# A graph network's gather stages: DVE reads one operand from PSUM beside the gathers, and POOL copies its own index columns

## The reference

```python
x = _layernorm(x + L0(x, ...)); x = _layernorm(x + L1(x, ...))
x = _layernorm(x + L2(x, ...)); x = _layernorm(x + L3(x, ...))
# L0, twice, with loops added: x = 0.5 * segment_sum(norm[:, None] * x[src], dst, n) + 0.5 * h; then relu, @ w1.T + b1, @ w2.T + b2
# L1: d_e = segment_sum(ones, he_idx, M);  d_v = segment_sum(hyperedge_weight[he_idx], node_idx, n)
#     he_feat = segment_sum(x_prime[node_idx], he_idx, M) * (hyperedge_weight / d_e)[:, None]
#     out = segment_sum(he_feat[he_idx], node_idx, n) * d_v_inv_sqrt[:, None];  return out @ W.T + b     (node_idx = src, he_idx = dst)
# L2: side = segment_sum(edge_weight[:, None] * emb[dst], src, n);  return (emb + 3 * side) / 4
# L3: edge scores from x[src], x[dst] and edge_attr, softmax over all edges, local[src] -= alpha * x[dst]
```

## Time and profile before

| | us |
|---|---|
| median of 3 runs (lowest, highest) | 8925.08 (8912.57, 8938.14) |
| the profiled execution | 8925.21 |
| its span | 8923.4 |
| PE busy | 4351.0 |
| PEld busy (beside PE) | 3221.3 |
| DVE busy | 3499.0 |
| ACT busy | 1201.9 |
| POOL busy | 5327.6 |
| POOL in the gathers of L368 | 3720.2 |

### The profile page before, as it was taken

How to read it: one execution, slowest core, us unless ns; L and a number is a source line. 1 busy time by engine, 2 the same in 40 slices (tenths; PEclk the granted TensorE clock), 3 DMA queues, 4 the chain that set the end, 5 groups by cost and what they waited for, 6 DMA issues and landing times. The chain is left out here.

```text
span 8923.4 us, 102562 instructions
## 1 busy us (share of the span) xinstructions
PE 4351.0 (49%) x17220; PEld 3221.3 (36%) x17221; DVE 3499.0 (39%) x11515; ACT 1201.9 (13%) x4632; POOL 5327.6 (60%) x5326
## 2 busy tenths in 40 slices
PE   6455554555543333145555555543333335666665
PEld 3333332333333323133333333322222224666654
DVE  8444444332232222141122222343333355666666
ACT  0000000000000000120000000010000024444443
POOL 0566675777776666626666666646666625555551
PEclk5555555555555555565555555555555558888886
DMA  9111111111111111161111211121111123333332
GB/s 159 52 45 46 44 46 45 45 46 46 45 45 45 46 44 45 42 38 45 45 44 45 45 44 45 45 42 44 44 44 44 43 48 93 96 98 99 98 94 40
DMA packets 665641, 492.66 MB, mean 55 GB/s; under 512 B 515113, under 2 KB 565684, under 8 KB 665476
## 3 DMA queue, kind: packets, MB, share of 16 engines
q0 software_dynamic: 183232, 378.81, 16.5%
q1 hardware_dynamic: 482228, 112.18, 7.6%
q10 hardware_dynamic: 144, 1.28, 0.1%
HBM read 411.96 MB, written 79.95 MB: 55 GB/s over the span
## 5 line engine op out<-in xcount | busy, mean ns | idle before, releaser
L368 POOL DMA_INDIRECT gathered<-node_table,idx x3696 | 3720.2, 1007 | 2151.6 <-issue 1124.8
L387 PE MATMUL ps<-onehots,gathered 128*128 128x128 f32 x4128 | 1618.6, 498 | 1484.4 <-DMA gathered<-node_table,idx 1336.3
L387 PEld LDWEIGHTS ps<-onehots,gathered 128*128 128x128 f32 x4128 | 1029.4, 312 | 2073.3 <-DMA gathered<-node_table,idx 1940.5
L389 PE MATMUL ps<-onehots,gathered 128*128 128x128 f32 x3264 | 1066.4, 470 | 1423.4 <-DVE agg L454 669.0
L389 PEld LDWEIGHTS ps<-onehots,gathered 128*128 128x128 f32 x3264 | 771.4, 319 | 1719.1 <-issue 907.3
L410 DVE TENSOR_TENSOR onehots<-iota,off_t 128x512 f32<-128x512 f32 x736 | 508.9, 693 | 2220.6 <-PE ps L387 1083.9
L923 POOL DMA_INDIRECT gathered<-node_table_xq,idx x832 | 796.1, 957 | 738.5 <-issue 225.9
L613 POOL DMA_INDIRECT bucketed_edges<-edge_rows,idx x782 | 775.6, 992 | 403.0 <-issue 253.1
L454 DVE TENSOR_TENSOR agg<-agg,ps 128x128 f32 x1632 | 466.9, 286 | 707.0 <-issue 608.7
L662 PE MATMUL ps<-gathered 128*128 128x49 f32 x1568 | 346.1, 414 | 681.9 <-DVE gathered L647 529.6
L662 PEld LDWEIGHTS ps<-gathered 128*128 128x128 f32 x1568 | 338.1, 332 | 689.8 <-DVE gathered L647 534.5
(11 more groups left out here) (258 smaller groups left out, 4482.7 us busy)
## 6 DMA issues: line engine op xcount, KB each, us to landing
gathered<-node_table,idx POOLq DMA_INDIRECT x3696
bucketed_edges<-edge_rows SPq DMA_DIRECT2D x52, 544.0 KB
edge_rows<-bucketed_edges SPq DMA_DIRECT2D x208, 128.0 KB
edge_rows<-in_edge_attr_dram SPq DMA_DIRECT2D x192, 128.0 KB
gathered<-node_table_xq,idx POOLq DMA_INDIRECT x832
bucketed_edges<-edge_rows,idx POOLq DMA_INDIRECT x782
node_table<-t_nodes SPq DMA_DIRECT2D x3, 3136.0 KB
node_table<-x_nodes SPq DMA_DIRECT2D x1, 3136.0 KB
```

The costliest lines, as they stand in the source:

```text
L368: nc.gpsimd.indirect_dma_start(g[:, k, :], None, table, bass.IndirectOffsetOnAxis(m.idx[:, k:k + 1], 0)).then_inc(S["landed"][k], 16)
L387: last = nc.tensor.matmul(m.ps[:, q, 0:P], g[:, k, :], m.oh[:, k, :], start=e == 0, stop=e == G - 1)
L389: last = nc.tensor.matmul(m.ps[:, q, e * P:(e + 1) * P], g[:, k, :], m.oh[:, k, :], start=True, stop=True)
```

## The change

DVE's operations beside the gathers read one of their two tensors from PSUM. `aggregate` copies `iota` once into the last 128 columns of bank 7, and L410 reads it there. In hop1 the hyperedges' weights are copied into banks 2 to 7 before the loop and read there by the side work, with a second load of the windows' starts into registers for it, clamped to M (written once per round, next to L424); PE then has two banks for its sums in place of four (`NS`). In hop2 the scan reads its ones from bank 7 and writes its running sum to banks 4 and 5, from where the predicated copy reads it.

ACT has no part in the loop any more. POOL casts eight index columns at a time itself (`stage`), twice per iteration, for the half that comes next: ahead of the fifth gather of each half it waits for `used` to say that PE has done the quarter four gathers back, and at the start of each half for its own copy. The clamp of the members' indices is computed once ahead of the stage, into `m.start`. The remaining hunks (sizes of a few tensors, and a loop register, `made`, that is now worked out where it is used) follow from this and are left out.

```diff
...
-def window_starts(nc, engine, m, at, count):
-    return nc.values_load_multi_w_load_instructions(m.startI[0:1, bass.ds(at, count)], engines=[engine], min_val=0, max_val=PARK,
-                                                    skip_runtime_bounds_check_because="clamped to PARK")[1]
+def window_starts(nc, engine, m, at, count, most=PARK):
+    return nc.values_load_multi_w_load_instructions(m.startI[0:1, bass.ds(at, count)], engines=[engine], min_val=0, max_val=most,
+                                                    skip_runtime_bounds_check_because="clamped to it")[1]
...
-def aggregate(nc, m, a, name, table, idx, dst_order, iters, weight=None, side=None, last_he=False, meta=None):
+def aggregate(nc, m, a, name, table, idx, dst_order, iters, weight=None, side=None, meta=None):
     off, NQ = m.off, U // G
+    NS = side.sums if side else NQ
     g = m.gather[:, 0:U * D].rearrange("p (t d) -> p t d", d=D)
-    with phase(nc, name, f"landed*{U} idx_ready used onehot added round dve side picked reg meta") as (S, block):
+    with phase(nc, name, f"landed*{U} idx_ready used onehot added round dve side picked meta") as (S, block):
         def iterations(eng):
             if isinstance(iters, int):
...
                                  a.bucketed[t0 * P:(t0 + n) * P, DE:DE + 3].rearrange("(t p) d -> p t d", p=P)).then_inc(S["meta"], 16)
                 sp.wait_ge(S["meta"], 16 * META)
-        @block.scalar
-        def _(act):
-            def body(t0, n, nt, i, made):
-                for q in range(NQ):
-                    cols, here = bass.ds(t0 + G * q, G), slice(G * q, G * q + G)
-                    act.wait_ge(S["used"], n * NQ + q + 1)
-                    if last_he:
-                        nc.scalar.activation(m.clampf[:, here], idx[:, cols], ACT.Relu, scale=-1.0, bias=m.lasthe[:, 0:1]).then_inc(S["reg"], 1)
-                        act.wait_ge(S["reg"], n * NQ + q + 1)
-                        nc.scalar.activation(m.idx[:, here], m.clampf[:, here], ACT.Identity, scale=-1.0,
-                                             bias=m.lasthe[:, 0:1]).then_inc(S["idx_ready"], 1)
-                    else:
-                        nc.scalar.copy(m.idx[:, here], idx[:, cols]).then_inc(S["idx_ready"], 1)
-            loops(act, body)
         @block.gpsimd
         def _(pool):
-            def body(t0, n, nt, i, made):
-                for q in range(NQ):
-                    hold(pool, S["idx_ready"], n * NQ + q + 1)
-                    for k in range(G * q, G * q + G):
+            pool.sem_inc(S["idx_ready"], 1)
+            def stage(t0, h):
+                cols, here = bass.ds(t0 + HALF * h, HALF), slice(HALF * (h % 2), HALF * (h % 2) + HALF)
+                nc.gpsimd.tensor_copy(m.idx[:, here], idx[:, cols]).then_inc(S["idx_ready"], 1)
+            def head(r, n):
+                if n is not None:
+                    hold(pool, S["idx_ready"], n * 2 + r + 1)
+                    hold(pool, S["used"], n * NQ + 2)
+                stage(0, 0)
+            def body(t0, n, nt, i, r):
+                for h in range(2):
+                    hold(pool, S["idx_ready"], n * 2 + r + h + 2)
+                    for k in range(HALF * h, HALF * h + HALF):
+                        if k == HALF * h + G:
+                            hold(pool, S["used"], n * NQ + 2 * h + 4)
+                            stage(t0, h + 1)
                         nc.gpsimd.indirect_dma_start(g[:, k, :], None, table,
                                                      bass.IndirectOffsetOnAxis(m.idx[:, k:k + 1], 0)).then_inc(S["landed"][k], 16)
-            loops(pool, body)
+            loops(pool, body, head)
         @block.tensor
         def _(pe):
             pe.sem_inc(S["used"], NQ)
-            def body(t0, n, nt, i, made):
+            def body(t0, n, nt, i, r):
                 for k in range(U):
                     q, e = k // G, k % G
                     if e == 0:
-                        pe.wait_ge(S["onehot"], made + q + 1)
+                        pe.wait_ge(S["onehot"], (n + r) * NQ + q + 1)
                         if dst_order:
                             pe.wait_ge(S["added"], n * NQ + q + 1)
                         else:
                             pe.wait_ge(S["added"], nt + G * q + G)
                     pe.wait_ge(S["landed"][k], nt + 16)
                     if dst_order:
-                        last = nc.tensor.matmul(m.ps[:, q, 0:P], g[:, k, :], m.oh[:, k, :], start=e == 0, stop=e == G - 1)
+                        last = nc.tensor.matmul(m.ps[:, q % NS, 0:P], g[:, k, :], m.oh[:, k, :], start=e == 0, stop=e == G - 1)
                     else:
                         last = nc.tensor.matmul(m.ps[:, q, e * P:(e + 1) * P], g[:, k, :], m.oh[:, k, :], start=True, stop=True)
                     if e == G - 1:
...
         @block.vector
         def _(v):
             V = nc.vector
-            a0 = NQ if dst_order else U
+            a0 = NS if dst_order else U
             v.sem_inc(S["added"], a0)
             step = chain(v, S["dve"])
+            step(V.tensor_copy(m.ps[:, 7, 512 - P:512], m.iota[:, :]))
             if side:
                 side.before(v, step, S)
             if dst_order:
...
                 here = m.oh[:, G * q:G * q + G, :]
                 if weight is None:
-                    V.tensor_tensor(here, m.iota[:, :].unsqueeze(1).to_broadcast([P, G, P]),
+                    V.tensor_tensor(here, m.ps[:, 7, 512 - P:512].unsqueeze(1).to_broadcast([P, G, P]),
                                     off[:, bass.ds(t0 + G * q, G)].unsqueeze(2).to_broadcast([P, G, P]), ALU.is_equal).then_inc(S["onehot"], 1)
                     return
                 for e in range(G):
...
                 if dst_order:
                     gs = m.glast[:, :]
                     V.tensor_scalar(gs, m.gstart[:, :], m.shift[:, 0:1], float(PARK), ALU.add, ALU.min).then_inc(S["round"], 1)
-                    v.wait_ge(S["round"], r * 4 + 1)
+                    v.wait_ge(S["round"], r * 5 + 1)
                     V.tensor_copy(m.startI[0:1, 0:NG], gs[0:1, :]).then_inc(S["round"], 1)
+                    V.tensor_scalar(m.startI[0:1, NG:2 * NG], gs[0:1, :], float(M), None, ALU.min).then_inc(S["round"], 1)
                     V.tensor_tensor(off[:, 0:NT].rearrange("p (t g) -> p t g", g=G), m.dst[:, 0:NT].rearrange("p (t g) -> p t g", g=G),
                                     gs.unsqueeze(2).to_broadcast([P, NG, G]), ALU.subtract).then_inc(S["round"], 1)
                     V.tensor_scalar(m.shift[:, :], m.shift[:, :], float(WIN), None, ALU.add).then_inc(S["round"], 1)
-                    hold(v, S["round"], r * 4 + 4)
+                    hold(v, S["round"], r * 5 + 5)
                 for q in range(NQ):
                     if dst_order:
                         v.wait_ge(S["used"], n * NQ + q + 1)
                     onehots(0, q)
-            def body(t0, n, nt, i, made):
+            def body(t0, n, nt, i, r):
                 if dst_order:
                     start = window_starts(nc, mybir.EngineType.DVE, m, i * NQ, NQ)
                 else:
                     start = window_starts(nc, mybir.EngineType.DVE, m, t0, U)
                 if side:
-                    for q in range(NQ):
-                        side.quarter(v, n, q, start[q], made, S)
+                    side.quarters(v, n, i, (n + r) * NQ, S)
                 for q in range(NQ):
                     v.wait_ge(S["used"], n * NQ + q + 1 + NQ)
...
                     if dst_order:
                         v.wait_ge(S["added"], n * NQ + q + a0)
                         w = m.agg[:, bass.ds(start[q], WIN)]
-                        V.tensor_tensor(w, w, m.ps[:, q, 0:P], ALU.add).then_inc(S["added"], 1)
+                        V.tensor_tensor(w, w, m.ps[:, q % NS, 0:P], ALU.add).then_inc(S["added"], 1)
                         continue
                     for e in range(G):
                         v.wait_ge(S["added"], nt + G * q + e + a0)
...
     def __init__(self, nc, m):
         self.nc, self.m = nc, m
+        self.sums = 2
+        self.cols = M + WIN
+        self.hw = m.ps[:, 2:8, :].rearrange("p b n -> p (b n)")[:, 0:self.cols]
     def before(self, v, step, S):
-        pass
-    def quarter(self, v, n, q, start, made, S):
+        m, V = self.m, self.nc.vector
+        for k in range(0, self.cols, 512):
+            w = min(512, self.cols - k)
+            step(V.tensor_copy(self.hw[:, k:k + w], m.side[:, k:k + w]))
+    def quarters(self, v, n, i, made, S):
         m, V, NQ = self.m, self.nc.vector, U // G
-        v.wait_ge(S["onehot"], made + q + 1)
-        V.tensor_tensor(m.junk[:, :, :], m.oh[:, G * q:G * q + G, :],
-                        m.side[:, bass.ds(start, WIN)].unsqueeze(1).to_broadcast([P, G, WIN]), ALU.mult).then_inc(S["picked"], 1)
-        v.wait_ge(S["picked"], n * 2 * NQ + 2 * q + 1)
-        V.tensor_reduce(m.picked[:, G * q:G * q + G], m.junk[:, :, :], AX.X, ALU.add).then_inc(S["picked"], 1)
```

(24 more changed lines are left out.)

19 lines of the change are left out of this document (9 added, 10 removed).

## The result

| | before | changed |
|---|---|---|
| median us (lowest to highest) | 8919.26 (8888.58 to 8938.14) | 8944.39 (8932.29 to 8963.0) |
| ratio, 95% interval | | 1.0026 (1.0019 to 1.0033) |
| ratio in a second comparison (run `after_again`) | | 1.0006 (0.9996 to 1.0016) |
| profiled span | 8923.4 | 8946.5 |

The account below looks back on a forecast made before the run. POOL's gathers were taken to bound the kernel: a 4609 us floor, 220 us of stretch, 539 us of pauses. The terms, -210 + 92 + 0 + 0 + 40 + 8 = -70 us, gave 8855 us, range 8480 to 9180.

Parts of the forecast that it names:

- What bounds the kernel: In the five gather stages, POOL's 3696 gathers set a floor of 4609 us, with stretched gathers and pauses above it.
- stretch: Gathers in the five stages taking longer than 0.947 us, mostly beside DVE operations with two SBUF tensors: 220 us together.
- pauses: POOL's waits for ACT's index copy in the five stages, less each stage's long first wait: 539 us in 165 waits.
- part 1: One-hots, weight products and scan read one tensor from SBUF, so gathers are no longer stretched: -210 us.
- rival C: In the gather stages something sets the pace; pauses grow by what the stretch loses: 8925 to 8990 us, chance 0.17.
- The copies: POOL's 462 index copies between gathers, 0.2 us each by a memset row, bounds 0.1 and 0.5: +92 us.
- ACT out of the loop: ACT's 0.19 us index copy leaves the path, but POOL's own wait, copy and issue take about as long: 0 us.
- The closer waits: POOL waits mid-half for PE's gather 4 places back, leaving 2.6 us of slack of some 13: 0 us.
- Rival B: Late signals to POOL end by themselves, so POOL stands up to 10 us longer each time: 9150 us, chance 0.20.
- hop2 loses a relief: In hop2 the scan's 1.4 us stops of POOL let things catch up; without them 0 to +74, taken +40 us.
- Once per stage: Copies of weights before hop1's first one-hot, copies of iota and two operations on the windows: +8 us.
- Rival D: Moving DVE's operands to PSUM does not free the gathers: 8855 + 210 = 9065 us, chance 0.05.

Follow-up runs that it names:

- after_again: The changed kernel unaltered, run again on the same chip as another run for comparing stages: 8943.09 us, 1.0006 of the kernel before.
- e1_psum_reads_only: The changed kernel with ACT's index copies and waits put back, so only the PSUM operands differ from the kernel before: 8939.13 us, ratio 1.0008.
- e2_pool_copies_only: The changed kernel with operands back in SBUF and four sums in hop1, so only POOL's index copies and their waits differ from before: 8934.81 us, ratio 1.0008.
- e5_wait_ten_back: The changed kernel, but POOL copies four columns per quarter, waiting for the quarter that ended 10 gathers back, not 4: 8921.89 us, ratio 0.9996.

## Why the prediction was wrong, point by point

- **What bounds the kernel** was half right. POOL's gathers are where the time is, but 4609 us of gathers, 220 of stretch and 539 of pauses are not three terms that can be taken away one by one. The last two are one term, what a pace of about 1.44 us a gather leaves over POOL's own work. The failing step is the sum of part 1: the stretch was sized right (211.7 us measured, 210 forecast) and priced as if it were on the path alone. `e1_psum_reads_only` shows it by itself: 223 us less in the gathers, 231 us more in the waits. The prediction had named the sign, a sum of pauses that moves by more than 100 us: POOL's waits went from 539 to 665 us, and with the gaps that the profile calls issue it was 209 us more.
- The page's numbers had said so. I wrote under rival C that the time per gather was about 1.44 us in hop1 and hop2 in spite of very different shares, and gave it 0.17. It was 1.448, 1.436, 1.434, 1.462 and 1.495 us in the five stages, while the stretch went from 0.6 to 124 us. Rival C, 8925 to 8990 us, is what came (8944), with a smaller price for the copies.
- **The copies** were 3 times too dear: 0.06 us each where nothing is late, 28 us in all, not 92, and below the lower bound of 0.1 too; in `e2_pool_copies_only`, with its copies and its stretch, the median is 7 us above the one before, which isn't clear of noise. The memset row gave the duration (0.13; the cast takes 0.19), but most of it fits into the issue gap, which I had put into the lower bound and not into the value.
- **ACT out of the loop**, 0: nothing speaks against it, and no run isolates it; `e1_psum_reads_only`, with ACT back in the loop and no copies on POOL, is at 1.0008 where the changed kernel is at 1.0026 and 1.0006. **The closer waits**, 0: right within 0.1 to 0.3%, which `e5_wait_ten_back` is faster than the changed kernel. The reason given, that running dry ends the delay, fits the traces and isn't proved by them. Rival B falls: by it each pause was to be up to 10 us longer, and the pauses got shorter, 3.7 us at most in hop1 where they were 5.6, and more frequent.
- **hop2 loses a relief**: right in kind, too small. Its waits rose from 22 to 128 us, not to hop1's 96, and cancelled its stretch of 124 us to within 5 us of stage time. Had I carried this part's own reading (a stop of POOL lets things catch up) to the stretches of the other stages, the -210 us would have been cancelled in the sum, as in rival C.
- **Once per stage**, 8 us: outside the five stages the changed profile has 8 us more, but two traces of one kernel differ by 13 and 19 us there. The two sums of hop1 were to cost nothing in an undisturbed iteration; hop1 is the one stage that got longer by more than 3 us both times, by 10 and 12, and 48 of its 49 iterations are disturbed. That the two sums do it is argued, as said above.
- **Rival D** falls: reading PSUM does free the gathers, 1.26 us before and 0.95 after beside the same one-hot (the earlier trace rows and the timeline of the changed kernel). The Trainium skill, "SBUF — State Buffer", § Who interferes with whom, has the rule that a DVE instruction with two SBUF inputs contends with a GpSimd instruction that reads SBUF, and these rows agree with it. The same section of the Trainium skill infers that tensor_tensor doesn't stall descriptor generation, and the same rows disagree.
